# Integer row indices in the tile buffer: the result scatter reads them there, and a buffer is reloaded when that scatter has landed

## The reference, cut to what matters

```python
logits = xf @ router_w
gate_vals, idx = jax.lax.top_k(logits, 2)          # 2 of 8 experts per token
gates = softmax(gate_vals)
for e in range(8):
    h = relu(xf @ w1[e] + b1[e]) @ w2[e] + b2[e]   # 128 -> 512 -> 128
    y = _layernorm(xf + h, gamma[e], beta[e])
    out = out + w_e[:, None] * y                   # w_e: the gate of the tokens that chose e
```

## Time and profile before

| | |
|---|---|
| time, median of 3 runs | 934.31 us (933.13 to 937.79) |
| the profiled execution | 936.52 us, of which the span is 934.7 us |
| busy: PE, DVE, ACT, POOL | 801.3, 761.1, 570.1, 501.4 us |
| expert phase | from 555 us (first load) to about 902 us (last scatter) |
| granted TensorE clock, mean | 0.952 |

### The profile page before, as it was taken

The page is one execution under the profiler, slowest core; times in us unless marked ns, Lnnn a source line. Parts: engine busy times, 40 slices in busy tenths (PEclk is TensorE's granted clock), DMA queues, the critical chain, the costliest instruction groups (busy, mean ns, idle before and its releaser), DMA issues.

```text
span 934.7 us, 27895 instructions
## 1 busy us (share of the span) xinstructions
PE 801.3 (86%) x7821; PEld 677.8 (73%) x7822; DVE 761.1 (81%) x3194; ACT 570.1 (61%) x1536; POOL 501.4 (54%) x660
## 2 busy tenths in 40 slices
PE   0698999889999999999999549999999999999910
PEld 0698999866677777777776428988888889988810
DVE  1668878834789989999989546999999999999987
ACT  2443334025899999999998406666666666666510
POOL 3000000000177888887788764677777777877750
PEclk9999999998999999999999569999999999999965
DMA  8634430053012121212121138222222222322389
GB/s 147 133 63 88 88 62 2 1 146 115 23 53 62 53 62 57 61 56 62 54 62 56 58 92 301 71 73 70 70 75 70 70 73 66 85 70 69 115 291 379
DMA packets 68634, 84.19 MB, mean 90 GB/s; under 512 B 12115, under 2 KB 52742, under 8 KB 68154
## 3 DMA queue, kind: packets, MB, share of 16 engines
q1 hardware_dynamic: 52727, 53.27, 21.7%
q0 software_dynamic: 12256, 22.50, 7.7%
q10 hardware_dynamic: 3555, 7.23, 2.4%
HBM read 48.15 MB, written 35.71 MB: 90 GB/s over the span
## 4 chain that ended last, share of the span: by engine, by line
PE 57%; DVE 21%; issue 9%; DMA 4%; ACT 4%; SPq 2%; DVEq 1%; ACTq 1%; POOL 1%; POOLq 0%
PE ps L694 9%; PE ps L953 8%; PE ps L794 5%; DVE arena L1063 4%; PE ps L769 3%; DVE arena L1397 3%; PE ps L780 3%; PE ps L843 3%; PE ps L942 3%; PE ps L829 3%; PE ps L848 2%; PE ps L775 2%; PE ps L862 2%; PE ps L944 2%; PE ps L943 2%
## 5 line engine op out<-in xcount | busy, mean ns | idle before, releaser
L605 POOL DMA_INDIRECT y_tokens<-arena x184 | 183.7, 998 | 84.2 <-DVE arena L1418 42.5
L578 POOL DMA_INDIRECT x_slots<-arena x192 | 190.6, 993 | 58.1 <-POOL arena L576 45.4
L953 PE MATMUL ps<-arena 128*128 x1472 | 180.6, 276 | 0.2 <-ACT arena L1660 0.2
L953 PEld LDWEIGHTS ps<-arena 128*128 128x128 f32 x1472 | 171.6, 192 | 1.6 <-issue 0.3
L1660 ACT ACTIVATE arena<-ps,b_t 128x256 f32<-128x256 f32 x368 | 144.2, 474 | 27.1 <-issue 14.9
L694 PE MATMUL ps<-wt,arena 128*128 128x128 f32 x960 | 118.0, 280 | 12.0 <-DVE arena L1063 12.0
L694 PEld LDWEIGHTS ps<-wt,arena 128*128 128x128 f32 x960 | 112.7, 195 | 13.4 <-DVE arena L1063 13.4
L942 PE MATMUL ps<-arena 128*128 128x256 f16 x368 | 101.3, 275 | 13.0 <-DVE arena L1366 10.2
L583 POOL MEMSET arena<- 128x258 f32 x1 | 0.3, 317 | 194.2 <-DVE arena L1314 194.2
L943 PE MATMUL ps<-arena 128*128 128x256 f16 x368 | 100.9, 274 | 0.0
L944 PE MATMUL ps<-arena 128*128 128x256 f16 x368 | 100.8, 274 | 0.0
(11 more groups left out here) (216 smaller groups left out, 1811.3 us busy)
## 6 DMA issues: line engine op xcount, KB each, us to landing
arena<-x_slots SPq DMA_DIRECT2D x92, 130.0 KB, 2.3
h<-h_rows SPq DMA_DIRECT2D x1, 5440.0 KB
arena<-y_tokens SPq DMA_DIRECT2D x17, 320.0 KB
out<-h ACTq DMA_DIRECT2D x17, 320.0 KB, 3.5
arena<-x_in SPq DMA_DIRECT2D x64, 84.5 KB
arena<-x_in SPq DMA_DIRECT2D x56, 78.0 KB
h_rows<-h SPq DMA_DIRECT2D x32, 128.0 KB
arena<-y_tokens SPq DMA_DIRECT2D x1, 3200.0 KB, 15.0
```

Of the source, the lines that this page charges most:

```text
L578: pool.indirect_dma_start(xs_dram, bass.IndirectOffsetOnAxis(ap=slot_i[n][0:rows, t, k:k + 1], axis=0), row[n][0:rows, k, t, :], None).the ...
L605: pool.indirect_dma_start(y_dram, bass.IndirectOffsetOnAxis(ap=y_id[n % YBUF][:, k:k + 1], axis=0), y_sl[n % YBUF][:, k, :], None, bounds_ ...
L953: ins = pe.matmul(ps[6 + m][:, 128 * k:128 * k + 128], hid[m][:, c, 128 * k:128 * k + 128], w2_sb[:, bass.ds(e, 1), c, :].rearrange("p o n ...
```

## The change

Word 129 becomes an integer. `row_i`, `pad_row_i` and `x_sl_i` are the same SBUF words as `row`, `pad_row` and `x_sl`, seen as int32. VectorE's two instructions that write word 129 (L1269, L1278) write integers, and so does the memset of the pad rows. The scatter of the results takes its indices from `x_sl_i[n]`, the tile's input buffer, and `y_id` with its cast (L1415) is gone. Since the scatter now reads the input buffer, `load(i)` waits for `y_gone` of tile i-8, that is until both scatters of that tile have landed.

```diff
-            def load(i, n):
-                need(sp, S["y_ready"], i - XBUF + 1)
+            def load(i, n, u):
+                if not isinstance(i, int) or i >= XBUF:
+                    sp.wait_ge(y_gone[n % YBUF], 32 * (XBUF // YBUF * u + n // YBUF) - 32 * (XBUF // YBUF - 1))
...
-            pool.memset(pad_row[:, :, 129:130], float(PAD_ID)).then_inc(S["pad_ready"], 1)
+            pool.memset(pad_row_i[:, :, 129:130], PAD_ID).then_inc(S["pad_ready"], 1)
...
-                        y_dram, bass.IndirectOffsetOnAxis(ap=y_id[n % YBUF][:, k:k + 1], axis=0),
+                        y_dram, bass.IndirectOffsetOnAxis(ap=x_sl_i[n][:, k, E_DIM + 1:E_DIM + 2], axis=0),
...
-                dve.scalar_tensor_tensor(row[p % ROWS][:, 0, :, 129], swap[:, :], float(NTOK), ids[:, 0, :],
+                dve.scalar_tensor_tensor(row_i[p % ROWS][:, 0, :, 129], swap[:, :], float(NTOK), ids[:, 0, :],
...
                 need(dve, y_gone[n % YBUF], 32 * (XBUF // YBUF * u + n // YBUF))
-                ch.step(dve.tensor_copy(y_id[n % YBUF], x_sl[n][:, :, E_DIM + 1]))
```

More of the change, by code:

```diff
@@ L258, in build @@
         rs2, rstd2, nb2 = A1.take(PTILES), A1.take(PTILES), A1.take(PTILES)
+        AI = Arena()
+        AI.at = A1.at
         row = [A1.take(2, PTILES, XW) for _ in range(ROWS)]
+        row_i = [AI.take(2, PTILES, XW, dt=I32) for _ in range(ROWS)]
         xn2_t = A1.take(PCOLS)
@@ L274, in build @@
         pad_i = A1.take(NEXP, dt=I32)
+        AI.at = A1.at
         pad_row = A1.take(2, XW)
+        pad_row_i = AI.take(2, XW, dt=I32)
         more, ntiles, tile_end, skip = A1.take(NEXP, 43), A1.take(NEXP), A1.take(NEXP), A1.take(NEXP)
@@ L288, in build @@
         A3.at = at - NEXP * FF
+        AI.at = A3.at
         x_sl = [A3.take(2, XW) for _ in range(XBUF)]
+        x_sl_i = [AI.take(2, XW, dt=I32) for _ in range(XBUF)]
         x_hi, x_lo = [A3.take(SLOT, dt=F16) for _ in range(2)], [A3.take(SLOT, dt=F16) for _ in range(2)]
@@ L303, in build @@
         bns3, mv3, ln3, rstd3, rg3 = (A3.take(2, 6), A3.take(2, 2), A3.take(2), A3.take(2), A3.take(2))
-        y_id = [A3.take(2, dt=I32) for _ in range(YBUF)]
         y_low = [A3.take(SUM_ROWS, E_DIM) for _ in range(NSUM)]
@@ L449, in expert_sync @@
             for n in range(XBUF):
-                load(n, n)
+                load(n, n, 0)
             sp.wait_ge(S["h1_stored"], 32 * PAIRS)
@@ L454, in expert_sync @@
                 for n in range(XBUF):
-                    load(XBUF * u + n, n)
+                    load(XBUF * u + n, n, u)
             for i in range(NTILE // XBUF * XBUF, NTILE):
-                load(i, i % XBUF)
+                load(i, i % XBUF, i // XBUF)
             y_half = y_dram.rearrange("(k p j) n -> k p j n", k=2, p=128)
@@ L1277, in gates @@
                 ch.step(dve.reciprocal(row[p % ROWS][:, 0, :, 128], den[:, :]))
-                dve.scalar_tensor_tensor(row[p % ROWS][:, 1, :, 129], swap[:, :], -float(NTOK), ids[:, 1, :],
+                dve.scalar_tensor_tensor(row_i[p % ROWS][:, 1, :, 129], swap[:, :], -float(NTOK), ids[:, 1, :],
                                          ALU.mult, ALU.add).then_inc(S["gate_done"], 1)
@@ L1682, in _ @@
             act.wait_ge(S["h_out"], 16 * NSUM)
-DVE_TILE = 5
+DVE_TILE = 4
 N_WLOADS = 2 + 7 + 1
```

## The result

| | before | after |
|---|---|---|
| time, median of 6 runs each | 935.47 us (929.66 to 937.79) | 946.77 us (944.83 to 950.45) |
| profiled execution, span | 936.52, 934.7 us | 949.1, 947.3 us |
| busy: PE, DVE | 801.3, 761.1 us | 814.7, 754.2 us |
| granted TensorE clock, mean | 0.952 | 0.939 |

The ratio is 1.013, 95% interval 1.0095 to 1.0165. The forecast was 936.5 with a range up to 946, so the median lies 0.8 us outside it on the slow side. The rival called "slower" gave 947.

What follows compares the result with a forecast made beforehand. PE, DVE and POOL lay within 0.4 us, the DVE-POOL phase deciding the pace. From 936.5 profiled, -3.1 (stretches), +2.4 (first reload), +3.0 (late landings) gave 938.8; with the median 2.2 lower, 936.5 us, 8-in-10 range 928 to 946.

Steps and rivals of the forecast that it cites:

- rival called "slower": Loop keeps old hold-ups, 14.5 per four tiles, if transposed input comes too late for L1373; about 947 us, chance 0.35.
- The bound and the loop: Expert phase: PE, DVE, POOL within 0.4 us; new scatter-to-reload loop over four tiles, 12.55 without hold-ups, 3.4 per tile taken.
- The example: Tile 46's scatter, tile 54's reload, L1373 of tile 51: the wait just fits, with 0.1 us to spare.
- The head of a pass: Register loads at each pass's head: mean price 1.4 us, making a stretch of eight 28.6, ten 3.1 us less.
- The cast: DVE without the cast ahead of L1418: 0.08 us less per tile, 0 to 7.4 us saved in all.
- What the 0.08 can do beyond its size: Moving DVE against POOL so slow stretches turn fast: gain bounded by 1.2 us for each of five stretches, 6 us.
- The integers and the indices: Type of word 129 and memset writes, and POOL's index reads from x_sl: taken as 0.
- The first reload: Tile 8's load waits for tile 0's scatter beside the 5440 KB transfer: +2.4 us, up to 3.2 late.
- The clock's fall: In the slower rival: PE's longer wait before tile 8 may again bring a clock loss of 1.2 us.
- Late landings: Scatters landing late in a loop without slack: three cases at 1 us, +3.0, bounds 0 and 6.
- slow kind: Stretches of eight tiles lasting about 29.35 us before, 3.60 per tile, with DVE held up beside POOL.
- fast kind: Stretches of eight tiles lasting about 28.16 us before, 3.23 per tile, POOL going round without a gap.

Runs made afterwards that it cites:

- e10: Kernel before with the register load at each head issued twice; the second load is not in the trace, so it repeats the kernel before; ratio 1.0137.
- e1: Kernel before with only the changed load wait (landed scatter of tile i-8); cast, y_id and floats stay; 952.01 us, ratio 1.0188.
- e17: Changed kernel with passes of 16 tiles in place of 8 for steps 16 to 79; 1015.68 us, ratio 1.0292, on a slower chip.
- e6: Kernel before with each reload waiting for VectorE's tile i-7 in place of i-8, without any landing; ratio 1.0063, on a slower chip.
- e13: Changed kernel with SP's read of the tile's place moved ahead of the wait on y_gone; 1017.8 us, ratio 1.0187, on a slower chip.
- e14: Changed kernel with eight extra thrown-away f32 matmuls on PE ahead of tile 8's transpose; ratio 1.0332, on a slower chip.
- e18: Kernel before with passes of 16 tiles in place of 8 for steps 16 to 79; 1003.4 us, ratio 1.0159, on a slower chip.
- e3: Kernel before with the index cast moved from VectorE to ScalarE, without the wait on a landing; 936.62 us, ratio 1.0018.
- e2: Changed kernel with integers travelling, but the index copy on VectorE and the load's wait as before; 936.09 us, ratio 1.0015.
- e7: Changed kernel with the 5440 KB transfer issued behind 16 loads in place of 8; ratio 1.0399, on a slower chip.
- e11: Kernel before with 12 input buffers and passes of 12 tiles; ratio 1.0006, on a slower chip.
- e12: Changed kernel with 12 input buffers and passes of 12 tiles, load(i) waiting for the landed scatter of tile i-12; ratio 1.0062, on a slower chip.
- e8: Changed kernel with the register load at each head issued twice; the second load is not in the trace, so it repeats the changed kernel; ratio 1.034.

## Why the prediction was wrong, step by step

**The bound and the loop: right.** Steady time was set by three engines within 0.4 us of each other, and the new loop was drawn link by link. Its links came out near what was taken: landing 2.25, SP 0.82 to 0.84, load 2.2, PE 2.4 (2.2 taken). Between heads four tiles take 13.24 in the median, 3.31 each; 3.4 was forecast. The example fitted as well, with more room than the 0.1 of the forecast: L1380 of tile 51 did not wait.

**The head of a pass: this step failed.** The prediction said: "With the mean, 1.4, a stretch takes 28.6." It took the head's price from a kernel in which nobody waited for the reload, and added it to the loop as if it stayed the same. Measured, a turn across a head takes 16.15 and one between heads 13.24: 2.9, not 1.4 (before: 15.28 and 13.78, thus 1.5). That is 1.5 more per stretch; the tiles themselves ran at 3.31 and not 3.4, which gives 0.7 back. The 0.8 that is left makes a stretch 29.4, and 8 us over ten, where stretches and late cases together were missed by 6.5 (6.4 measured, -0.1 forecast).

VectorE's own stop at a head is not what grew. It was there before, and on the chain of waits: at all eight steady heads in e10, at four of eight in the profiled execution of the kernel before, at seven of eight in the changed one. The first row is a steady head before, the other three are the changed kernel from a head on, in the order of time:

```profile
703.16 0.42 DVE L1366 TENSOR_TENSOR arena<-ps,arena 128x256 f16<-128x256 f32 x1 [1.62 <-ACT arena L1652]
...
710.16 0.42 DVE L1373 TENSOR_TENSOR arena<-ps,arena 128x256 f16<-128x256 f32 x1 [1.09 <-PE ps L951]
...
714.25 1.01 POOL L612 DMA_INDIRECT y_tokens<-arena  x1 [2.04 <-DVE arena L1424]
...
720.91 0.44 PE L934 MATMUL ps<-cst,arena 128*128 128x128 f32 x2 [1.22 <-DMA arena<-x_slots]
```

VectorE stands idle 1.62 at the head before and 1.09 now. What is new is what follows. Behind the stop VectorE writes the result of tile 36, whose scatter POOL then starts late. The reload for tile 44 waits for that scatter, and PE waits 1.22 for the reload. The pattern repeats with every pass: from tile 30 to tile 84 PE waits more than half a microsecond for a load only at tiles 36, 44, 52 and so on up to 84 (0.8 to 1.6 us each), and in e1 at the same tiles. The kernel before has no such wait; there these loads had 2.7 us to spare, and the lateness ended with them. So the head's lateness now goes round the loop once more and reaches PE, a path that a fixed 1.4 per head did not contain. That it is the head which makes these waits is read from where they stand, and no run shows it by itself. In e17, which has a stall of its own at each jump, they stand at tiles 44 and 60, where no head is ahead of them, and not at 36 and 52, where one is.

e6 raises the turn across a head from 15.36 to 15.98 by lateness alone, and e13 has 15.4 in place of e14's 16.5 by earliness. At the missing heads of e17 and e18 the price differs by 0.8 or so. How much of the 1.5 is PE's wait for the reload, and how much is anything else at the head, was not measured; PE's own register load is on the chain at no steady head.

**The cast: the bounds held, the use did not.** e3 shows 0 without the wait; after against e1, 4.3 us in the ten stretches and 5.2 in the time, within the 0 to 7.4. "What the 0.08 can do beyond its size", to turn slow stretches into fast ones, happened nowhere. The Trainium skill (SBUF — State Buffer, two physically separate sides) has a VectorE instruction with two SBUF inputs and a GpSimd instruction that reads SBUF take the shared port pair in turn. By that rule the hold belongs to L1424 itself, whatever stands ahead of it; the mean of 481 ns for L1424, the same as for L1418 before, agrees.

**The integers and the indices: right**, 0 by e2 within 0.4%, and L612's mean of 1003 ns where L605's was 998.

**The first reload: mechanism right, size low.** Forecast +2.4, and +4.6 measured for the start. The load of tile 8 landed at 586.28, beyond the forecast's 585.1 to 585.6; the scatter took 5.3 to land. e7 takes the transfer away and with it 3.8 us of the start. The clock's fall, named in the rival, seems to be 0.4 to 1.6 us of it and of the first stretch. The kernels with the old wait start in 31.4 to 33.6, so a part of the 4.6 may be chance.

**Late landings: the count right, the price not measured.** Three cases of 1 us were an estimate. From tile 4 on, three scatters for which a reload waits landed over 1.9 us after their end (tiles 12, 15 and 83, where the median is 1.35), and one load took 3.72. Behind the first PE waited 1.75 at tile 20, about 0.5 more than usual. POOL's pause at tile 56, which is no DMA at all and stood in no term, added 0.9 us.

**The sum.** Predicted for start, stretches and late cases: 2.4 - 3.1 + 3.0 = +2.3. Measured: 4.6 + 6.4 = +11.0, and 0.6 behind them. The rival "slower" came near in the stretches: "The fast stretches then rise to 29.35 (+4.4 in sum), the start costs 3.2". Three of them rose by 4.6 and the start cost 4.6. The prediction gave it 0.35. But its loop of 14.5 per four tiles everywhere was not there (13.24 and 16.15), and its late landings of 3 to 6 us were not seen as such, so that its 947 is in part luck. Its condition was a transposed input later than L1380 can wait. In the slow kind the forecast's example, which fitted by 0.1, is no exception, but it was done there alone. The same working in the fast kind, for tile 72, would have met the condition in the trace of the kernel before:

```profile
808.43 0.98 POOL L605 DMA_INDIRECT y_tokens<-arena  x1 [0.30 <-issue]
...
815.12 0.41 DVE L1373 TENSOR_TENSOR arena<-ps,arena 128x256 f32<-128x256 f32 x1
```

From the second scatter of tile 64 at 808.43, the 2.3, 0.83, 2.3 and 2.17 of the forecast give 816.03 for the input of L1373 of tile 69, which started at 815.12. Most tiles from 62 to 80 come out so, 0.7 to 0.9 too late. It is this fast kind that is gone.

The Trainium skill (DMA: Bandwidth & Descriptors, Anatomy of one DMA) spoke against the change: it puts most of the fixed 2 us of a DMA issued by GpSimd into the confirmation of the write. The scatter is such a DMA; the load is issued by SP. The trace agrees with the total, 2.25 and 2.17 in a row; how much of it is the confirmation, no run here shows. With more tiles in the loop no loss against e11 is left in e12.

## What to carry to other kernels

A buffer that is freed by a DMA's landing in place of an engine's last instruction needs more room. Here the reload is issued a median of 5.8 us after the end of VectorE's last instruction, where it was 0.8: compare such a difference with the least slack of any load in the trace, and if nothing is left, price it as a loss. When slack goes, lateness that used to end at a buffer (behind the stop at a loop's head, a rare pause of one engine, SP's address read) can be handed on to the next engine; don't carry its old price over. An instruction saved on an engine that is held up by another is worth nothing until something downstream waits for it.

## What was not expected of the hardware

- A loop body twice as long brought 2.4 to 3.0 us without a reason in the trace at each of VectorE's jumps back (e17, e18); with 8 tiles in the body, in the kernel before, it was at most 0.3.
- A load of one register takes 0.27 us (SP's L452), of 16 registers 1.10, of 24 registers 1.6. The Trainium skill (Runtime: NRT & Kernel Launch, the preamble/postamble breakdown) has about 1.3 us for the register loads of the preamble, which come from HBM. The table here lies in SBUF, so that figure does not price it.
- POOL paused between the two scatters of tile 56 in all twenty profiled kernels, with 8, 12 or 16 tiles in a pass, and at no other tile for as long: the distance was 2.5 to 3.2 us where 1.3 is usual.
- The time from a landing to SP's next issue differed between chips, 0.82 against 1.10 to 1.36 us in the median, but where PE waited for a load, the time from scatter to transpose was nearly the same, 4.36 against 4.35 to 4.47 us (e14, e8, e7).
